# Another order for the seven up products of a pair, with the routed products ahead of them, in a one-core attention and feed-forward kernel

## What is computed

```
x = x + attention(layernorm(x), ctx_4096, Wq, Wk, Wv, Wo)
logits = x @ gate_w;  routing_weights, _ = top_k(logits, 2)
h = relu(x @ up_w) ** 2                                   # 1024 -> 2048
shared_out = h @ down_w                                   # 2048 -> 1024
x_latent = x @ fc1_w;  expert_out = x_latent @ expert_w
routed_out = (expert_out * sum(routing_weights)) @ fc2_w
x = x + layernorm_affine(shared_out + routed_out, gamma, beta)
```

## Time and profile before

| | us |
|---|---|
| median of 3 runs | 1735.61 |
| time of the profiled execution | 1735.55 |
| its span | 1733.8 |
| PE busy in the span | 1705.7 (98%) |
| up stage with the routed products, first product to the start of the down stage | 1410.41 to 1587.74 |

### The profile page before, as it was taken

The page is one execution under the profiler, slowest core; times in us unless marked ns, Lnnn a source line. Parts: engine busy times, 40 slices in busy tenths (PEclk is TensorE's granted clock), DMA queues, the critical chain, the costliest instruction groups (busy, mean ns, idle before and its releaser), DMA issues.

```text
span 1733.8 us, 24758 instructions
## 1 busy us (share of the span) xinstructions
PE 1705.7 (98%) x8539; PEld 1502.7 (87%) x8539; DVE 1026.1 (59%) x1520; ACT 736.5 (42%) x1409; POOL 961.6 (55%) x775
## 2 busy tenths in 40 slices
PE   9999999999999999999999999999999999889998
PEld 8988998899999988888988898889888987777887
DVE  3711112743434458875877577757657366866998
ACT  3311212233434357734773477247513224445342
POOL 2365553445555549875767576736534244555565
PEclk9999999999999999999999999999999999999999
DMA  8788876566677669834763476334223105643344
GB/s 271 227 285 284 295 246 214 171 195 219 207 225 247 218 208 303 290 121 142 249 219 121 149 243 211 116 102 152 82 81 113 55 31 175 220 147 97 133 145 158
DMA packets 214295, 319.37 MB, mean 184 GB/s; under 512 B 20304, under 2 KB 174416, under 8 KB 213328
## 3 DMA queue, kind: packets, MB, share of 16 engines
q1 hardware_dynamic: 214224, 318.49, 56.6%
HBM read 211.78 MB, written 106.66 MB: 184 GB/s over the span
## 4 chain that ended last, share of the span: by engine, by line
PE 90%; DVE 3%; POOL 3%; DMA 2%; issue 1%; ACT 1%; SPq 0%; DVEq 0%; POOLq 0%; ACTq 0%
PE bank L2289 28%; PE bank L2290 28%; PE bank L2291 28%; PE bank L2513 5%; POOL slab_raw L1186 1%; DMA slab_raw<-in_slabs 1%; PE bank L2375 1%; POOL tile_region_rounded L1195 1%; DVE act_region_unrounded L2105 1%; POOL act_region L1195 0%; DMA mid_region<-k_latents_scratch 0%; DVE tile_region L2105 0%; PE bank L2654 0%; PE bank L2361 0%; DVE slab_split_unrounded L2125 0%
## 5 line engine op out<-in xcount | busy, mean ns | idle before, releaser
L1102 POOL TENSOR_TENSOR tile_region<-tile_region,small 128x487 f32<-128x487 f32 x224 | 221.1, 1024 | 73.2 <-DVE small L1787 73.1
L2289 PE MATMUL bank<-mid_region 125*128 125x448 f32 (+4 forms) x608 | 248.3, 408 | 0.5 <-DMA mid_region<-k_latents_scratch 0.3
L2290 PE MATMUL bank<-mid_region 125*128 125x448 f32 (+4 forms) x608 | 229.4, 377 | 0.0
L2291 PE MATMUL bank<-mid_region 128*128 128x488 f32 (+4 forms) x572 | 215.0, 376 | 0.0
L2289 PE MATMUL bank<-mid_region,act_region 128*125 128x512 f32 (+3 forms) x434 | 168.5, 388 | 1.7 <-POOL act_region L1195 1.7
L2290 PE MATMUL bank<-mid_region,act_region 128*125 128x512 f32 (+3 forms) x434 | 168.3, 388 | 0.0
L1372 ACT ACTIVATE tile_region<-bank,small 128x487 f32<-128x487 f32 x224 | 153.8, 687 | 30.3 <-DVE small L1791 30.3
L1068 POOL TENSOR_TENSOR slab_raw<-slab_raw 128x256 f32<-128x256 f32 x128 | 98.4, 771 | 120.0 <-DMA slab_raw<-in_slabs 112.5
L1404 ACT ACTIVATE mid_region<-bank 125x512 fp32r<-125x512 f32 x224 | 136.7, 613 | 54.7 <-PE bank L2513 54.7
L1791 DVE TENSOR_REDUCE small<-bank 128x1 f32<-128x487 f32 x224 | 146.0, 653 | 20.8 <-PE bank L2291 20.8
L1842 DVE TENSOR_TENSOR mid_region<-bank,mid_region 125x512 fp32r<-125x512 f32 x224 | 151.8, 683 | 9.3 <-ACT mid_region L1404 9.3
(11 more groups left out here) (310 smaller groups left out, 4290.7 us busy)
## 6 DMA issues: line engine op xcount, KB each, us to landing
slab_raw<-in_slabs SPq DMA_DIRECT2D x112, 256.0 KB, 3.8
q_scratch<-y_region SPq DMA_DIRECT2D x16, 1792.0 KB, 8.1
mid_region<-q_scratch SPq DMA_DIRECT2D x32, 896.0 KB, 7.1
slab_raw<-in_slabs SPq DMA_DIRECT2D x48, 512.0 KB, 3.5
weight_sums_scratch<-slab_raw SPq DMA_DIRECT2D x32, 512.0 KB, 4.4
small_region_unrounded<-in_slabs SPq DMA_DIRECT2D x52, 256.0 KB, 4.8
v_scratch<-slab_split SPq DMA_DIRECT2D x8, 1536.0 KB, 7.7
slab_raw<-weight_sums_scratch SPq DMA_DIRECT2D x48, 256.0 KB, 4.5
```

What stands on the lines that cost most here:

```text
L1102: pool.tensor_tensor(PR[i][:, 0:KEYS], PR[i][:, 0:KEYS], rrow[:, i:i + 1].broadcast_to([P, KEYS]), ALU.mult).then_inc(s_pn, 1)
L2289: pe.matmul(out_ap, w[0], a[0], start=first, stop=False)
L2290: pe.matmul(out_ap, w[1], a[0], start=False, stop=False)
L2291: return pe.matmul(out_ap, w[0], a[1], start=False, stop=last)
```

## The change

- `F_BLOCKS` becomes A22, A11, S1, S2, A12, S3, S4. S3 = A22-S2 is now written where S1 (A21) stood, no longer over S2.
- POOL's list per pair becomes: lo of 0, lo of 1, sum 1, lo of 2, sum 2, sum 3, lo of 3, (wait for DVE's lo of 4), sum 4, lo of 6. As many instructions as before.
- SP loads A22 of the next pair behind sum 3, A11 behind sum 4, A21 behind DVE's lo of 5, A12 behind the lo of 6.
- ACT copies products 0 and 1 out of their banks (one copy more per pair, 8 in all), and always makes the hi of unit u+3 behind product u. Two of the four tiles of h are done behind product 5, the others behind 4 and 6.
- DVE makes no combination behind products 1 and 2: three behind product 3, one behind 4, two behind 5, one behind 6. Seven as before.
- PE: products 4 and 5 wait for the two copies, product 6 for combination 3; products 0 to 2 of the next pair for combinations 4, 6 and 7.
- The 16 sets of down sums move to 3, 4, 4, 2, 2, 1 in pairs 0 to 5, all behind products 0, 1, 2 and 6.
- The seven routed products run ahead of pair 0, not between its products; the last row sum (T4) is split meanwhile.
- On entering the down stage, `chunk_hi(0, 2)` moves up and two tiles of h instead of one stand ahead of `down_hi(0)`; some regions are placed anew.

```diff
-F_BLOCKS = ("A11", "S2", "A12", "S3", "S1", "A22", "S4")
+F_BLOCKS = ("A22", "A11", "S1", "S2", "A12", "S3", "S4")
...
-ROUTED_WEAVE = (2, 2, 1, 1, 1, 0, 0)
...
-CHUNKS = ((1, 0, "Y"), (1, 1, "X"), (1, 3, "Z"), (1, 4, "V"), (1, 6, "Y"), (2, 0, "X"), (2, 3, "Z"), (2, 4, "V"),
-          (2, 6, "X"), (3, 0, "Y"), (3, 3, "Z"), (3, 5, "X"), (3, 6, "Y"), (4, 4, "X"), (4, 6, "Y"), (5, 5, "Y"))
+CHUNKS = ((0, 1, "X"), (0, 2, "Y"), (0, 6, "Z"), (1, 0, "V"), (1, 1, "X"), (1, 2, "Y"), (1, 6, "Z"), (2, 0, "V"),
+          (2, 1, "X"), (2, 2, "Y"), (2, 6, "Z"), (3, 1, "X"), (3, 2, "Y"), (4, 1, "X"), (4, 2, "Y"), (5, 2, "Y"))
...
                     if more and n == 2:
-                        sp.wait_ge(s_ulo, lo_count(p, 3))
+                        sp.wait_ge(s_usum, 4 * p + 3)
+                        load_up(p + 1, "A22")
+                    if more and n == 4:
+                        sp.wait_ge(s_usum, 4 * p + 4)
                         load_up(p + 1, "A11")
-                    if more and n == 3:
-                        sp.wait_ge(s_ulo2, 2 * p + 1)
+                        sp.wait_ge(s_ulo2, 2 * p + 2)
                         load_up(p + 1, "A21")
...
             for p in range(F_PAIRS):
+                up_lo(p, 0)
+                up_lo(p, 1)
                 up_sum(1, p, "A21", "A21", "A22", ALU.add)
-                up_lo(p, 0)
+                up_lo(p, 2)
                 up_sum(2, p, "A11", "A21", "A11", ALU.subtract)
-                up_lo(p, 1)
-                up_lo(p, 2)
-                up_sum(3, p, "A12", "A12", "A11", ALU.subtract)
-                up_sum(4, p, "A11", "A22", "A11", ALU.subtract)
+                up_sum(3, p, "A21", "A22", "A11", ALU.subtract)
                 up_lo(p, 3)
+                pool.wait_ge(s_ulo2, 2 * p + 1)
+                up_sum(4, p, "A12", "A12", "A11", ALU.subtract)
                 up_lo(p, 6)
...
-                    for v in (u + 2,) if u < 5 else (7, 8) if u == 5 else (u + 3,):
-                        if v < UNITS:
-                            up_hi(v // 7, v % 7)
...
+                        act.activation((F_P4, F_P1)[n], UB[n][:, 0:HALF], ACT.Copy).then_inc(s_first_p, 1)
+                    if u + 3 < UNITS:
+                        up_hi((u + 3) // 7, (u + 3) % 7)
...
+                    if n == 4:
+                        hidden_block(p, 0)
+                    if n == 5:
+                        hidden_block(p, 1)
+                        hidden_block(p, 2)
                     if last and n == 5:
                         down_hi(0)
-            chunk_hi(0, 2)
+                    if n == 6:
+                        hidden_block(p, 3)
+            chunk_hi(0, 3)
...
                     if n == 3:
-                        up_combine(p, 3, n, F_U3, F_U, ALU.add)
...
+                        up_combine(p, 1, n, F_U, F_P1, UB[3], ALU.add)
+                        up_combine(p, 2, n, F_P4, F_U, F_P4, ALU.subtract)
+                        up_combine(p, 3, n, F_U, F_U, UB[2], ALU.add)
+                    if n == 4:
+                        up_combine(p, 4, n, F_P1, F_P1, UB[0], ALU.add)
                     if n == 5:
-                        up_combine(p, 6, n, F_SUM, F_U3, ALU.subtract)
+                        up_combine(p, 5, n, F_SUM, F_U, UB[1], ALU.add)
+                        up_combine(p, 6, n, F_P4, F_P4, UB[1], ALU.add)
                     if n == 6:
-                        up_combine(p, 7, n, F_SUM, F_U, ALU.add)
...
+                    if n in (1, 2):
+                        up_lo(p, n + 3)
...
+                if n in (4, 5):
+                    pe.wait_ge(s_first_p, 2 * p + n - 3)
+                if n == 6:
+                    pe.wait_ge(s_upc, 7 * p + 3)
+                if p > 0 and n < 4:
+                    pe.wait_ge(s_upc, 7 * (p - 1) + (4, 6, 7, 1)[n])
...
+            for r in range(RT):
+                routed_product(C_FFN + r, r)
             for p in range(F_PAIRS):
                 for n in range(7):
                     up_product(p, n)
-                    for c, r in woven(p, n):
-                        routed_product(c, r)
```

More of the change, by code:

```diff
@@ L326, in xattn_ffn @@
                   [part(FB_R, 2 * HALF, 512), part(FB_R, 3200, 512)]]
[L327 to L330, removed]
+        F_P4, F_U = [part(YR, RT * HID + i * HALF, HALF) for i in range(2)]
+        F_P1, F_SUM = [part(FB, i * HALF, HALF) for i in range(2)]
+        F_DONE = (F_P1, F_SUM, F_P4, F_U)
+        F_BLOCK = {name: part(RAW, i * 512, 512) for i, name in enumerate(("A22", "A11", "A21", "A12"))}
+        F_SRC = {"A11": "A11", "S2": "A11", "A12": "A12", "S3": "A21", "S1": "A21", "A22": "A22", "S4": "A12"}
         def split_at(region, at, n):
             return [part(region, at + l * n, n) for l in range(2)]
-        D_W = [split_at(RA, 2 * ROWS, SLAB), split_at(RB, 0, SLAB), split_at(RB, 7168, SLAB), split_at(RB, 12288, SLAB),
+        D_W = [split_at(RA, 4 * F_WORDS, SLAB), split_at(RB, 8704, SLAB), split_at(RA, 2 * F_WORDS, SLAB), split_at(RB, 3584, SLAB),
                split_at(RC, SLAB, SLAB)]
         D_OP = [split_at(t, at, 6 * P) for t, at in (
-            (RA, 3840), (RA, 5376), (RA, 6912), (RA, 8448), (RB, 2048), (RB, 3584), (RB, 5120), (RB, 10752))]
+            (RA, 9216), (RB, 0), (RB, 1536), (RB, 7168), (RA, 5632), (RB, 5632), (RB, 10752), (RB, 12288))]
         D_OP = [[t.rearrange("p (k n) -> p k n", k=2) for t in pair] for pair in D_OP]
-        D_RIDE = [[t.rearrange("p (k n) -> p k n", k=2) for t in split_at(RB, at, 2 * P)] for at in (9216, 9728, 10240, 6656)]
+        D_RIDE = [[t.rearrange("p (k n) -> p k n", k=2) for t in split_at(region, at, 2 * P)]
+                  for region, at in ((RB, 3072), (RA, 1792), (RA, 2304), (RA, 2816))]
         def raw_chunk(name, kp):
@@ L959, in _ @@
             sp.wait_ge(s_wlo, P_FFN)
-            for name in ("A11", "A21", "A22", "A12"):
+            for name in ("A22", "A11", "A21", "A12"):
                 load_up(0, name)
+            sp.wait_ge(s_ftlo, 4)
+            sp.wait_ge(s_mm, C_FFN + RT)
+            for c in range(4):
+                load_chunk(c)
             for p in range(F_PAIRS):
@@ L966, in _ @@
                     if more and n == 2:
-                        sp.wait_ge(s_ulo, lo_count(p, 3))
+                        sp.wait_ge(s_usum, 4 * p + 3)
+                        load_up(p + 1, "A22")
+                    if more and n == 4:
+                        sp.wait_ge(s_usum, 4 * p + 4)
                         load_up(p + 1, "A11")
-                    if more and n == 3:
-                        sp.wait_ge(s_ulo2, 2 * p + 1)
+                        sp.wait_ge(s_ulo2, 2 * p + 2)
                         load_up(p + 1, "A21")
-                    if more and n == 4:
-                        sp.wait_ge(s_ulo2, 2 * p + 2)
-                        load_up(p + 1, "A22")
                     if more and n == 5:
@@ L1534, in hidden_block @@
                 to = HR[p][:, m, h * HALF:(h + 1) * HALF]
-                act.activation(to, F_FIRST if n == 2 else F_SUM, ACT.Relu).then_inc(s_relu, 1)
+                act.activation(to, F_DONE[i], ACT.Relu).then_inc(s_relu, 1)
                 act.wait_ge(s_relu, 4 * p + i + 1)
```

111 lines of the change are left out of this document (37 added, 74 removed).

## The result

| | before | after |
|---|---|---|
| median of 10 runs, us | 1736.71 | 1740.68 |
| lowest to highest | 1735.61 to 1737.93 | 1739.42 to 1741.52 |
| profiled execution, its span | 1735.55, 1733.8 | 1740.49, 1738.5 |

The ratio is 1.0023 (95% interval 1.0014 to 1.0032): slower by 0.23%, where 1729.7 (1723.5 to 1739.5) and faster had been forecast. The median is 1.2 above the range.

What follows compares the result with a forecast made beforehand. PE was taken to lose 22.0 us in waits, mainly on POOL's chain and its loads. Of the pairs' 18.7, 12.0 of new waits and 0.9 at the entry left 5.8 won: 1735.55 - 5.8 = 1729.7 us, range 1723.5 to 1739.5.

Steps and rivals of the forecast that it cites:

- DVE's part of the sum: Pairs 0 to 5: combinations 1 to 3 behind up to two sets; seven waits, 10.6 us, 12.0 with restarts.
- the entry: Into the down stage: 4.2 us lost in place of 3.3, a loss of 0.9.
- A: Up stage: placing the sets saves nothing, each costs 3.62 us; pair 0 waits at product 6; 1738.8 us, chance 0.20.
- B: Up stage: combinations' delay is one wait; past 3.15 us the clock falls, 1.7 more each; 1753 us, chance 0.07.
- C: POOL's chain: product 3 takes over product 0's wait in every pair; 16 us lost, not 18.7; 1733.8, chance 0.13.
- The price of a set: DVE's down sums in the up stage: 2.9 us per set on average, against 3.62 in the rows; called the shakiest term.
- The blocking: POOL steps beside DVE sums: 0.06 to 0.1 us counted; waiting a whole sum, 0.43, would make the time 1732.
- The combinations: On DVE behind product 3: 0.62 us each, 0.57 when queued, one input in PSUM; three made from 12.6 to 14.3.
- Product 3 and product 6: PE waits: product 3 in pairs 1 to 5, 1.3 to 1.65 us; product 6 in pairs 1 and 2, 1.65 and 1.15.
- The clock: Behind the wait before the down stage: falls to 1.2 GHz again, worth 1.7 us, so no change.
- POOL's wait for loads: POOL in the up stage: its idle time for loads, 15.9 us in all, goes to near nothing.
- The price of a restart: PE after each of seven waits: 0.38 us each in the rows, 0.2 each added, making 12.0 us.

Runs made afterwards that it cites:

- The two moves: ACT's first down_w hi ahead of third chunk and two tiles, DVE's second-chunk lo behind last combination; changed kernel 1.0006, with PSUM-operand sums 0.9894.
- second version of the early split: Changed kernel, ACT's first down_w hi ahead of third chunk and two tiles, DVE's second-chunk lo behind last combination: 1737.82 against 1736.61 us.

## Why the prediction was wrong, step by step

**Where it missed.** The step that failed is DVE's part of the sum: its sets, lo steps and the block of three combinations were priced too low, so that the waits at product 6 in pairs 0, 3 and 4 and at product 5 were put at nothing. The time lost was to be 12.0 in the pairs and 4.2 at the entry; it was 22.1 and 4.6. The forecast waits in the pairs were seven, 10.6 us; there were twelve, 16.4 us. The prediction's own signs for A (pair 0 waits at product 6) and for B (the clock falls in the up stage) both came; that for C did not (product 3 waits 0.30 in pair 6 and not at all in pair 7).

| pair | 0 | 1 | 2 | 3 | 4 | 5 | 6 | 7 |
|---|---|---|---|---|---|---|---|---|
| predicted, us | 17.0 | 20.4 | 20.2 | 18.8 | 18.8 | 18.8 | 17.0 | 17.0 |
| measured | 18.2 | 22.1 | 24.0 | 19.5 | 20.9 | 18.6 | 17.8 | 17.3 |

**The price of a set** was the term that I called the shakiest, and it failed: 2.9 predicted, 3.40 measured, near the 3.62 of the earlier trace rows. I had placed eleven sets behind products 1 and 2, "where POOL waits for others". By the timeline these took 2.76 to 3.98, 3.1 on average, and the five behind products 6 and 0 took 3.83 to 4.97, 4.4 on average. DVE and POOL in pair 1 of the changed kernel (timelines; the first set is the one behind product 6 of pair 0):

```profile
1449.05 4.27 DVE L2094 TENSOR_TENSOR act_region_unrounded<-act_region_unrounded 128x256 f32<-128x256 f32 x4
1453.24 4.81 DVE L2094 TENSOR_TENSOR small_region_unrounded<-small_region_unrounded 128x256 f32<-128x256 f32 x4
1457.63 0.43 DVE L2094 TENSOR_TENSOR small_region_unrounded<-small_region_unrounded 128x256 f32<-128x256 f32 x1
...
1461.26 1.78 DVE L2083 TENSOR_TENSOR act_region<-slab_raw,act_region 128x512 fp32r<-128x512 f32 x1
...
1465.77 0.61 DVE L2076 TENSOR_TENSOR y_region<-tile_region,bank 128x448 f32<-128x448 f32 x1
1466.49 0.62 DVE L2076 TENSOR_TENSOR y_region<-y_region 128x448 f32<-128x448 f32 x1
```

```profile
1449.65 1.36 POOL L1174 TENSOR_TENSOR slab_raw<-slab_raw 128x512 f32<-128x512 f32 x1
1451.75 1.29 POOL L1183 TENSOR_TENSOR act_region<-slab_raw,act_region 128x512 fp32r<-128x512 f32 x1 [0.74 <-ACT act_region L1511]
1453.12 2.79 POOL L1174 TENSOR_TENSOR slab_raw<-slab_raw 128x512 f32<-128x512 f32 x2
1455.87 1.45 POOL L1183 TENSOR_TENSOR tile_region_rounded<-slab_raw,slab_split 128x512 fp32r<-128x512 f32 x1
```

The row of 1457.63 is the fourth subtraction of the set of 4.81. Where POOL runs on (1453.12 to 1457.3), the first three take 4.4: one sum for each POOL instruction. The fourth, with POOL idle, takes 0.43. The windows of pairs 1 and 2 (columns as above) show an engine that is full:

```profile
1448.30:1470.40 22.10, 17.87 (x85) 15.45 (x85) 20.57 (x25) 9.24 (x18) 12.30 (x10) 1.00 0.61 193
1470.40:1494.40 24.00, 19.52 (x86) 16.79 (x86) 20.26 (x25) 10.80 (x21) 13.77 (x11) 0.93 0.73 237
```

DVE is busy for 20.57 of 22.10. Rival A had put its load at 4 x 3.62 + 4.0 + 1.8 = 20.3. A's total of 1738.8 was the nearest of all, and I gave it 0.20. A has no fall of the clock in the stage, though, and no more than the forecast for the combinations.

**The blocking, charged in part.** Beside DVE's sums POOL's step took 1.36 to 1.45 rather than 1.29, so the small figure that I kept for POOL held within 0.06. My 2.9 per set already held 1.2 us of blocking above the 1.7 of four sums alone; the trace has 1.7 above it. The one set that I priced high, behind product 0 of pair 1, was near (5.2, measured 4.81). To DVE's lo steps and to combination 2 I charged none. The Trainium skill (SBUF — State Buffer, section "SBUF: two separate sides") says that of the two whichever starts first keeps the other out for its whole instruction. The trace agrees for DVE (0.42 alone, 1.5 each in those rows) and less for POOL, whose steps lost under 0.2 to sums of 0.42. By the same section of the Trainium skill the lock wants two SBUF operands on DVE. The runs with a PSUM operand bear this out: 0.42 again.

**The combinations.** I counted three in 1.7, at 0.57 each. Each waits for the one before it and they start 0.72 to 0.73 apart (1465.77, 1466.49), and combination 2 has both operands in SBUF, which I overlooked when I wrote that they have one in PSUM: it took 1.43 in pair 0, and 1.66 in the last pair, beside POOL, where alone it took 0.62. In pair 0 the block ran from 1442.86 to 1445.72, 2.9 us for 1.7. This and two sets at 2.77 each, for 2.3 and 2.6, are pair 0's 1.2. DVE's own lo steps, counted at 0.7 to 0.8, took 1.4 to 1.8 beside POOL. Product 5 waited in pairs 1 and 2, where I had no wait: in pair 1 its lo took 1.78, in pair 2 the lo took 0.68 and the set ahead of it was the long one (1481.09 to 1484.97, 3.88).

**Product 3 and product 6.** Product 3 was to wait 1.3 to 1.65 in pairs 1 to 5. It waited 1.61, 1.55, 1.29 and 1.29 in pairs 1, 2, 4 and 5 and not at all in pair 3, so this step held but for one pair. Product 6 waited 1.99 and 1.92 in pairs 1 and 2 (1.65 and 1.15 forecast), and 1.94 in pairs 3 and 4, where I had said that product 3's wait would cover it.

**The clock.** I had a fall only past a wait of 3.15, the one wait of the rows that had one behind it. Behind the wait of 1.92 in pair 2 the granted clock fell to the lower level (1.2 GHz) for part of two windows:

```profile
1490.00:1492.00 2.00, 1.71 (x5) 1.53 (x6) 1.69 (x4) 0.97 (x2) 0.00 (x0) 0.63 0.96 265
1492.00:1494.00 2.00, 2.00 (x7) 1.78 (x7) 0.41 (x1) 1.97 (x5) 1.22 (x1) 0.52 1.06 357
```

By their granted clock that is 2 x 0.37 + 2 x 0.48 = 1.7 us, of the 3.7 by which pair 2 was longer than forecast. It is rival B's mechanism, at a shorter wait.

**What held.** POOL's wait for loads went from 15.9 us to nothing; the routed products ahead cost PE nothing; the copies, SP's list and the changed queues held nobody up; pair 5 came within 0.3 and pairs 6 and 7 within 0.8. The price of a restart did not hold: before, 18.7 us were lost for fourteen waits of 14.5, not thirteen of 13.7, so 0.30 each and not 0.38. At the entry the cause and the size were right: 4.6 against 4.2, with its wait at 4.45. The two moves took the ratio from 1.0023 to 1.0006, some 2.9 us: more than the change had added there, since they cut the wait below the 3.15 of the earlier trace rows as well.

**The sum.** 22.0 - 12.0 - 4.2 = 5.8 won became 22.0 - 22.1 - 4.6 = -4.7. Of the 10.5 between them 1.7 are the clock and 0.4 the entry. Another 5.8 are longer waits (16.4 for 10.6), which come from DVE: sets, combination 2 and lo steps that POOL held up. The last 2.6 is time lost at the products beside what the view calls waiting: 1.4 were forecast and some 4 measured. The run without sums still lost 2.6 in this way with no wait at all, so most of this part is not the down sums'; the forecast charged it only where PE waits. That the blocking of the down sums is the main cause is shown by the runs in which only the operand's place changed; how the 5.8 divide among the three kinds is not.

## What to carry to other kernels

Before a reorder that relieves one engine, add up the load of the engine that comes next at its price in company, not alone: here a pair takes PE 17 us, and DVE, with four sets beside its own work, was busy for 20.6. Where GpSimd works beside VectorE, look for VectorE instructions with both operands in SBUF, and give them one in PSUM (a copy by an idle engine pays): that turned a loss of 0.2% into a gain of 0.8%, and of 1.1% with the two moves at the entry. When a change brings nothing, run both orders without the side work; the pair of runs shows at once whether the gain never came or was given back.

## What the runs showed of the hardware

- The price of blocking is uneven. Beside a run of POOL's steps DVE's 0.42 became 1.5 (the row of 4.81), and POOL's 1.3 became 1.45; beside a DVE lo step that started 0.03 before it POOL's took up to 1.81 (1561.67). Where a 0.95 DVE instruction had started first, POOL's 2.43 became 3.05.
- The clock fell behind waits of 1.92 (pair 2) and 2.19 (entry) and did not behind 1.99 (pair 1), 1.94 (pair 3) or 1.94 (pair 4). The window behind the 1.99:

```profile
1467.00:1472.00 5.00, 4.11 (x20) 3.82 (x21) 3.38 (x7) 3.31 (x7) 1.54 (x2) 1.00 1.03 343
```

- The code of the pairs does not decide it either. The second version of the early split has the same pairs 0 to 6 as the changed kernel. There the clock fell behind the 1.99 of pair 1, at the same product, and did not behind the 1.91 of pair 2. Its wait and the window behind it:

```profile
1468.94 0.47 PE L2271 MATMUL bank<-mid_region,slab_split 128*128 128x448 f32 x1 [1.99 <-DVE y_region L2075]
```

```profile
1470.00:1472.00 2.00, 2.00 (x8) 1.77 (x7) 0.96 (x2) 1.94 (x5) 0.57 (x1) 0.54 0.96 310
```

So behind a wait of about 2 us the clock fell in one execution and stayed up in the other at the same place; the two falls cost some 1.6 us each. What decides is open; the length of a wait alone does not.

- The entries with 4.45, 3.43 and 2.19 of waiting were each followed by a window at 0.50 to 0.55, in one profiled execution each, so that shortening the wait to 2.19 did not save the clock there.
